# A drain of TensorE in place of the product's own increment, each four products of an edge-count fill

## The reference, cut to what matters

```python
def _gcn_conv(z, W, b, row, col, n):
    norm = _gcn_norm(row, col, n)
    h = z @ W
    msg = h[row] * norm[:, None]
    return jax.ops.segment_sum(msg, col, num_segments=n) + b
...
edge_index = jnp.stack([src, dst])
x = x + _L1_gnn_ref(_layernorm(x, axis=-1), edge_index, ...)
```

## Time and profile before

| | us |
|---|---|
| median of three runs without the profiler | 5562.96 |
| span of the profiled execution | 6940.0 |
| preparation (0 to 311 of the profile) | 311 |
| count fill (311 to 2172) | 1861 |
| attention walk (2172 to 3861) | 1689 |
| first routed feed-forward (3861 to 4560) | 699 |
| convolutions (4560 to 5890) | 1330 |
| second routed feed-forward (5890 to the end) | 1050 |

### The profile page before, as it was taken

The page is one execution under the profiler, slowest core; times in us unless marked ns, Lnnn a source line. Parts: engine busy times, 40 slices in busy tenths (PEclk is TensorE's granted clock), DMA queues, the critical chain, the costliest instruction groups (busy, mean ns, idle before and its releaser), DMA issues. The chain is left out here.

```text
span 6940.0 us, 113554 instructions
## 1 busy us (share of the span) xinstructions
PE 4623.5 (67%) x23328; PEld 3590.1 (52%) x23329; DVE 3284.3 (47%) x10456; ACT 2960.7 (43%) x7576; POOL 2148.9 (31%) x2057
## 2 busy tenths in 40 slices
PE   2411111366565677777777479799999998369997
PEld 1300000233323555555555479677777776369997
DVE  6511111487666666666666745533334333522222
ACT  0200000266666555555555523256655665623332
POOL 2477777300002555555555222100000000422221
PEclk8655555698767888888888589899999999589999
DMA  4377676322224656665566456547753444556665
GB/s 131 113 212 199 193 202 194 116 89 95 95 93 131 165 164 166 169 168 167 163 167 166 127 162 181 146 145 223 221 177 93 133 134 117 165 155 181 181 181 168
DMA packets 623736, 1084.57 MB, mean 156 GB/s; under 512 B 74390, under 2 KB 502093, under 8 KB 616748
## 3 DMA queue, kind: packets, MB, share of 16 engines
q1 hardware_dynamic: 504252, 733.75, 35.3%
q0 software_dynamic: 112144, 268.88, 15.3%
q10 hardware_dynamic: 7200, 80.28, 2.8%
HBM read 782.21 MB, written 309.57 MB: 157 GB/s over the span
## 5 line engine op out<-in xcount | busy, mean ns | idle before, releaser
L740 POOL DMA_INDIRECT arena<-table,arena x1664 | 1667.0, 1002 | 1909.3 <-DVE arena L877 1481.3
L686 PE MATMUL banks<-arena 128*128 128x392 bf16 x2368 | 654.0, 432 | 1198.9 <-issue 846.0
L1416 PE MATMUL banks<-parts,a_wide 128*128 128x512 f32 x4900 | 1179.9, 399 | 17.9 <-ACT a_wide L1439 17.9
L940 PE MATMUL banks<-arena 128*128 128x261 f32 x3328 | 1157.6, 487 | 0.0
L686 PEld LDWEIGHTS banks<-arena 128*128 128x128 bf16 x2368 | 342.1, 151 | 1510.6 <-issue 1470.8
L1416 PEld LDWEIGHTS banks<-parts,a_wide 128*128 128x128 f32 x4900 | 918.3, 189 | 262.9 <-ACT a_wide L1439 47.2
L1439 ACT CAST a_wide<-arena 128x896 fp32r<-128x896 f16 x700 | 658.9, 942 | 421.8 <-PE banks L1416 407.0
L709 ACT CAST arena<-banks 128x1568 f16<-128x1568 f32 x200 | 293.1, 1465 | 1261.2 <-issue 716.9
L940 PEld LDWEIGHTS banks<-arena 128*128 128x128 f32 x3328 | 701.9, 234 | 87.1
L2344 ACT ACTIVATE rings<-banks,b_sb 128x128 f32<-128x128 f32 x1296 | 370.6, 369 | 827.8 <-PE banks L2377 827.7
L658 DVE TENSOR_TENSOR arena<-arena 128x1024 bf16<-128x1024 f16 x296 | 203.9, 689 | 1083.2 <-issue 597.6
(11 more groups left out here) (367 smaller groups left out, 5313.2 us busy)
## 6 DMA issues: line engine op xcount, KB each, us to landing
arena<-counts SPq DMA_DIRECT2D x700, 224.0 KB, 2.5
arena<-in_L_ffn_W SPq DMA_DIRECT2D x114, 1024.0 KB
edge_rows<-arena SPq DMA_DIRECT2D x364, 264.0 KB
arena<-edge_rows SPq DMA_DIRECT2D x364, 264.0 KB
counts<-arena ACTq DMA_DIRECT2D x50, 1568.0 KB
arena<-in_L_ffn_w SPq DMA_DIRECT2D x64, 1024.0 KB
arena<-near_rows SPq DMA_DIRECT2D x416, 128.0 KB
expert_in<-rings SPq DMA_DIRECT2D x25, 2028.0 KB
```

The source lines that it names most:

```text
L686: last = pe.matmul(psum_all[:, bass.ds(bank, KEYS)], oh_b[:, p // LB % (OR // LB), :, p % LB], oh_k[:, p // KB % (OR // KB), :, p % KB], s ...
L740: pool.indirect_dma_start(out=got[:, r, j, :], out_offset=None, in_=table0, in_offset=bass.IndirectOffsetOnAxis(ap=src_sb[:, 2 * pair + j: ...
L940: last = pe.matmul(banks_a[u][:, 0:mw], onehot[:, u % GS, j, :], msg[:, u % RB, j, 0:mw], start=False, stop=False, skip_group_check=True)
L1416: last = pe.matmul(psum[u][:, 0:2 * D], a_wide[:, at:at + P], parts[:, a * 2 * D:(a + 1) * 2 * D], start=(a == 0), stop=(a == NT - 1))
```

## The change

The product no longer carries the increment of `done`. After each fourth product TensorE's sequencer runs a drain, which holds the sequencer until TensorE has nothing in flight, and the drain increments `done`. Waits, counts, shapes and the order of the products stay as they were.

```diff
-                            last = pe.matmul(psum_all[:, bass.ds(bank, KEYS)], oh_b[:, p // LB % (OR // LB), :, p % LB],
-                                             oh_k[:, p // KB % (OR // KB), :, p % KB],
-                                             start=False, stop=False, skip_group_check=True)
+                            pe.matmul(psum_all[:, bass.ds(bank, KEYS)], oh_b[:, p // LB % (OR // LB), :, p % LB],
+                                      oh_k[:, p // KB % (OR // KB), :, p % KB],
+                                      start=False, stop=False, skip_group_check=True)
                             if p % PG == PG - 1:
-                                last.then_inc(done, 1)
+                                pe.drain().then_inc(done, 1)
```

## The result

The changed kernel takes 5966.12 us, the median of four runs (5953.37 to 5975.74), against 5562.05 us, by now a median of four runs too: a ratio of 1.0726 with a 95% interval of 1.0711 to 1.0742. It is slower, by 404 us, as forecast in sign; the forecast was 5690 us with a range up to 5830, and that is missed by 136 us.

A forecast was written before the change was run, and what follows sets the result against it. The prediction took the fill as what matters, with TensorE becoming slowest after the change. Boundaries of 100 us plus 30 us for the clock gave 5563 + 130 = 5693, taken as 5690 us, range 5552 to 5830.

The forecast's parts named there:

- The shape of the timed run: Kernel before, without the profiler: fill 984 us, ending at 1295 us, then walk 1189 us; the profile's slow part not in full.
- rival 1: Fill: late product-carried increments also slow the timed run, so the change makes it faster; halfway case 5397 us; chance 0.13.
- The boundary: Between two groups of four products in the fill: a drain costs 0.60 us where no wait covers it.
- The chain at full clock: TensorE in the fill: two steps, four groups with drains and one load, take 6.5 us, 3.25 us a step.
- The clock: Fill steps at VectorE's pace: near 0.3 of the time at 1.2 GHz, costing 30 us.
- The boundaries themselves, 100 us: Fill, drains between groups without the clock: 75 us early, 19 in the middle, 6 late, sum 100 us.
- The late part, 6 us: Late fill, 4.0 us a unit: TensorE's wait for ScalarE covers the drains, leaving 0.05 us on some 110 units, 6 us.
- The upper bound of 355 us: Whole fill: 592 boundaries at 0.60 us, all in the open, add 355 us, giving 5918 us.
- Rival 3: Fill: all boundaries in the open, clock at half for most of it, 250 to 355 us more, 5813 to 5918; chance 0.10.
- Rival 2: Fill: loss hidden because gathers end 100 us later, or boundaries fall into waits; 5563 to 5574 us; chance 0.09.

The follow-up runs named there:

- The second profile: The kernel before, unchanged, run and profiled once more: 5558.55 us, profiled span 5556.8 us.
- the twin with drains: The changed kernel with columns 196 to 391 of each product left out: 5681.98 us.
- the twins: The changed kernel and the kernel before, both with columns 196 to 391 of each product left out: 5681.98 and 5546.42 us.
- the carried twin: The kernel before, increments carried by products, with columns 196 to 391 of each product left out: 5546.42 us.
- The two faster fills: The kernel before with half of each product's columns left out, 5546.42 us, and with loads of 8 bank numbers in place of 16, 5543.6 us.
- loads of eight: The kernel before with 8 bank numbers loaded at each step in place of 16 at each second: 5543.6 us.

## Why the prediction was wrong, by its own steps

**The shape of the timed run: right.** From a profile that was 1377 us too long it took 984 us for the fill, 1189 for the walk and the fill's end at about 1295 us. The second profile has 1022 (1013 from first to last product), 1191 and 1294. That the end agrees to a microsecond is luck: the fill starts at 281 and not at 311, and takes some 30 us longer. The argument that the 22.4 us steps can't be in the timed runs held, and rival 1 with it fell.

**The boundary: right.** Predicted gap 0.05 + 0.33 = 0.38 us, measured 0.40; the starts across it at 1.2 GHz are 1.92 us apart for four products where seamless ones would take 4 x 0.33 = 1.32: 0.60 us, as in the sum. At 2.4 GHz it is 1.33 - 4 x 0.176 = 0.63. The drains end 0.02 us behind the fourth product's end, in the median of the 592; the first row below is theirs. Two items were missing: 0.11 us where the wait on `hot` stands, and the load beside gathers. I took 1.107 us from a stretch without them. In the kernel before, nearly all of whose fill runs beside them, the same instruction has a median of 1.5 us (second row, from its second profile):

```profile
L690 PEldq DRAIN  x592: 441/1170/1190, 281.2 to 1706.9; - x198
...
L648 PEldq TENSOR_LOAD <-arena x147: 1101/1497/4247, 284.0 to 1282.0; - x147
```

**The chain at full clock: right where no gathers run.** 6.5 us for 16 products predicted, 6.67 measured. Beside gathers the twin with drains, with products about as short, took 7.08.

**The step that failed: "The clock ... near 0.3 of the time at 1.2 GHz ... 30 us".** The changed fill was at 1.2 GHz for 0.9 of the time (0.55), where I had read 0.85 from the number of products per 100 us. This term, 30 us, is what the twins leave as some 232. VectorE's steps, which I had said would come 3.2 us apart, come 9.49 / 2 = 4.75 apart.

I had looked up the clock that a given rate of products goes with in the kernel before, where they come in runs of eight or sixteen. In bunches of four with gaps between, and at the lower rate that a low clock itself causes, it doesn't hold. Nor does it with other products: in its first 300 us the carried twin had 890 products of half the columns at 0.51, and the kernel before 880 whole ones at 0.94. With more drains the fill's clock goes down: 0.81 without, 0.76 with one in eight products, 0.55 with one in four. It isn't the number of drains alone: one in sixteen has 0.80 with the load ahead and 0.75 with the load behind, and one in four has 0.60 with the load ahead. That the low clock lowers the rate, and the lower rate keeps the clock low, is my reading of it; no run moved the one without the other. The changed fill settles at 500 products in 300 us:

```profile
281.00:581.00 300.00, 192.74 (x512) 74.62 (x510) 0.52 0.74 218
581.00:881.00 300.00, 183.23 (x503) 73.08 (x504) 0.56 0.81 252
881.00:1181.00 300.00, 179.42 (x497) 71.72 (x496) 0.57 0.83 265
1181.00:1481.00 300.00, 181.35 (x499) 72.09 (x498) 0.56 0.32 117
```

The same stretches of the kernel before, second profile:

```profile
281.00:581.00 300.00, 192.95 (x880) 121.69 (x878) 0.94 0.75 234
581.00:881.00 300.00, 181.70 (x680) 98.97 (x680) 0.79 0.85 278
881.00:1181.00 300.00, 173.88 (x596) 87.38 (x596) 0.72 0.87 289
```

The columns before and after tell the rest. Before, the rate falls as units get shorter and ScalarE sets the pace. After, it is nearly flat: the chain is the bound almost from the first product to the last.

**The boundaries themselves, 100 us: too small as well.** The prediction's own three stretches, by product number, from the starts of these products in the traces (us):

| products | predicted, without the clock | twins of half columns | changed kernel less kernel before |
|---|---|---|---|
| 1 to 928 | 75 | 104 | 227 |
| 929 to 1423 | 19 | 38 | 85 |
| 1424 to 2368 | 6 | 40 | 101 |
| all | 100 | 182 | 414 |

So two terms were mis-sized, 30 for 232 and 100 for 182, and the clock's is the larger miss by far.

**The late part, 6 us: wrong, and not by the clock alone.** I counted on ScalarE's 4.0 us a unit as cover. At 2.4 GHz the chain is 3.3 us a step where no gathers run, and fits under it; at 1.2 GHz it is 4.75 and doesn't. Of that cover only 122.9 us are left of 225.1. But with short products the twins lose 40 us here too, so the cover was less than I took it for. Why, stays open.

**The upper bound of 355 us was none.** It priced all boundaries in the open but left the products as long as they were. 592 x 0.60 plus what a lower clock does to the starts of 2368 products (0.33 for 0.176 us each, 365 us) would have been the bound, and held the 404.

**Rival 3, all in the open (0.10), had the mechanism.** It named TensorE's chain next to ScalarE's loop and a clock at half for most of the fill. Its price of 250 to 355 us ended at 5918, 48 us short of the measured time.

The Trainium skill, "PSUM — Partial Sum Buffer", section "Engine vs sequencer instructions", asks for the increment on the matmul as a matter of correctness and says that a drain waits for the engine to go fully idle. The drains here agree with the latter: 8 ns in the median where TensorE is empty, 960 ns where it isn't. What this waiting costs the page doesn't say; here it is 404 us for 592 drains.

**Rival 2, hidden,** fell too, but its mechanism is real: of the kept gathers and the walk's first eight together (736) the last starts at 1290.4 us in the kernel before, 3.5 us ahead of the fill's last product. The two faster fills gained only 16 to 18 us; a slower one is paid in full.

## What to carry to other kernels

A drain costs the overlap that it forbids, not its own few nanoseconds. Leave the increment on the product; where a drain is needed, put it where the engine is empty anyway, and count how late its increment then comes (34 us for 148 of them here). When an edit puts gaps between bunches of matmuls, work the sum out at both clocks and see which engine is the bound at each; don't take the clock from a table of rates measured with other bunches. And if a profiled span is far from the timed runs, profile the same kernel again before a number is taken from it.

## What was not expected of the hardware

In one profiled execution of the kernel before VectorE's steps came 22.4 us apart while GpSimd gathered. The recorded updates of `done` bear out the reading of late increments: the trace has 34 of them between 311 and 1303 us, most of them 11.2 us or a multiple of it apart. Eleven other profiled executions, seven of them with increments carried by some or all products, and the same kernel among them, have no such steps. What set it off stays open.

GpSimd's gathers end earlier beside a slower fill. The last of 736 starts at 1290.4 us beside the fill of the kernel before and at 1238.7 beside the slower one, whose median gather is 0.950 and not 1.125 us:

```profile
L740 POOL DMA_INDIRECT arena<-table,arena x736: 942/1125/3883, 241.3 to 1290.4; - x184
```

```profile
L740 POOL DMA_INDIRECT arena<-table,arena x736: 942/950/3883, 241.5 to 1238.7; - x184
```

What links the two isn't shown. It isn't VectorE's work alone: in the first profile, where VectorE was nearly idle, the median was 1.008 us and the 736 took 1016 us from first to last start, against 997 beside the changed fill and 1049 in the second profile. Beside the two faster fills the walk's first gather starts at 1282.8 us (half the columns) and 1280.2 (loads of eight), against 1279.7 in the kernel before, so these gathers set the walk's start there, and both stop at about 5545 us.
